# Latent attention: the plain f32 products of two head pairs together in every second slot, and the values of the latents in 64x64 tiles over two banks

## The reference

```python
x = layer_norm(image_embeds, ln1_g, ln1_b)      # the context, 256 rows
l = layer_norm(latents, ln2_g, ln2_b)           # the latents, 64 rows
q = l @ Wq
kv = concatenate([x, l], axis=1) @ Wkv          # 320 rows of keys and values
k, v = split(kv, 2, axis=-1)
w = softmax(einsum('bhqd,bhkd->bhqk', q * scale, k * scale))
out = einsum('bhqk,bhkd->bhqd', w, v)
return out @ Wo                                 # and x = x + this
```

## Time and profile before

| | us |
|---|---|
| median of 3 runs (2218.87 to 2220.65) | 2220.39 |
| the profiled execution | 2218.44 |
| its span, from the first to the last instruction | 2216.6 |
| PE busy in the span | 2118.9 |

### The profile page before, as it was taken

The page is one execution under the profiler, slowest core; times in us unless marked ns, Lnnn a source line. Parts: engine busy times, 40 slices in busy tenths (PEclk is TensorE's granted clock), DMA queues, the critical chain, the costliest instruction groups (busy, mean ns, idle before and its releaser), DMA issues.

```text
span 2216.6 us, 50712 instructions
## 1 busy us (share of the span) xinstructions
PE 2118.9 (96%) x20881; PEld 1883.0 (85%) x20881; DVE 1218.3 (55%) x3619; ACT 1157.9 (52%) x2620; POOL 502.8 (23%) x416
## 2 busy tenths in 40 slices
PE   6999999999999999699879999999999999999999
PEld 5899999998989998466758878878999999999998
DVE  5656565656555555657556777842874843342411
ACT  4656565656565555333237766653444444444443
POOL 0000011000000000122221221232444444444444
PEclk9999999999999999999989999998999999999999
DMA  4000200000000000000031100010101101011000
GB/s 143 21 16 21 72 21 16 23 15 28 18 18 20 16 6 1 11 1 1 1 116 31 31 26 27 12 40 1 58 1 39 39 1 39 1 39 38 1 10 29
DMA packets 48803, 58.08 MB, mean 26 GB/s; under 512 B 6528, under 2 KB 40128, under 8 KB 48448
## 3 DMA queue, kind: packets, MB, share of 16 engines
q1 hardware_dynamic: 48576, 54.85, 7.8%
HBM read 46.72 MB, written 2.10 MB: 22 GB/s over the span
## 4 chain that ended last, share of the span: by engine, by line
PE 45%; DVE 3%; issue 1%; ACT 1%; POOL 0%; POOLq 0%; DVEq 0%; ACTq 0%
PE bank L83 20%; PE bank L1031 16%; PE bank L969 3%; PE bank L955 2%; PE bank L942 1%; PE bank L910 1%; PE bank L978 1%; PE bank L997 1%; DVE dec_room L140 0%; DVE att_rden L1290 0%; DVE att_vz L1272 0%; PE bank L1002 0%; DVE dec_ts_rawa L113 0%; PE bank L901 0%; PE bank L990 0%
## 5 line engine op out<-in xcount | busy, mean ns | idle before, releaser
L861 POOL TENSOR_TENSOR moe_h<-moe_hr,moe_h 128x512 fp32r<-128x512 f32 x256 | 340.8, 1331 | 431.3 <-ACT moe_hr L1175 431.3
L1174 ACT ACTIVATE moe_h<-bank,dec_b 128x512 fp32r<-128x512 f32 x256 | 176.4, 689 | 401.5 <-PE bank L83 378.0
L83 PE MATMUL bank<-lat_wv,lat_kv_t 128*128 128x256 f32 (+1 forms) x1728 | 261.9, 301 | 8.7 <-DVE lat_wv L2188 4.9
L83 PE MATMUL bank<-lat_kv_t,lat_qk 128*128 128x320 f32 x1536 | 258.8, 317 | 0.0
L83 PEld LDWEIGHTS bank<-lat_wv,lat_kv_t 128*128 128x128 f32 x1728 | 224.4, 190 | 16.8 <-ACT lat_v L2096 5.7
L83 PEld LDWEIGHTS bank<-lat_kv_t,lat_qk 128*128 128x128 f32 x1536 | 225.2, 188 | 8.7
L2121 ACT ACTIVATE lat_p<-bank,lat_neg_max 128x320 f32<-128x320 f32 x256 | 135.2, 528 | 166.2 <-DVE lat_neg_max L2237 166.2
L2231 DVE TENSOR_TENSOR lat_qk<-bank,lat_qk 128x256 fp32r<-128x256 f32 x256 | 96.7, 420 | 197.6 <-ACT lat_qk L2115 197.4
L83 PE MATMUL bank<-dec_xt,dec_lo 128*128 128x512 f32 x512 | 202.5, 396 | 0.0
L2237 DVE TENSOR_REDUCE lat_neg_max<-bank 128x1 f32<-128x320 f32 x256 | 125.7, 492 | 132.3 <-PE bank L83 132.1
L1175 ACT ACTIVATE moe_hr<-bank,dec_b 128x512 f32<-128x512 f32 x256 | 174.6, 682 | 0.0
(11 more groups left out here) (321 smaller groups left out, 4060.3 us busy)
## 6 DMA issues: line engine op xcount, KB each, us to landing
raw_w<-in_L_ffn_W SPq DMA_DIRECT2D x16, 1024.0 KB, 6.4
lat_ctx_raw<-in_ctx SPq DMA_DIRECT2D x16, 512.0 KB, 4.0
att_ctx_raw<-in_ctx_turned SPq DMA_DIRECT2D x16, 512.0 KB, 3.7
lat_kv_t<-lat_lt SPq DMA_DIRECT2D x32, 128.0 KB, 2.1
out_x<-x_sb SPq DMA_DIRECT2D x4, 512.0 KB, 2.9
x_sb<-in_x SPq DMA_DIRECT2D x1, 1792.0 KB, 14.7
lat_xl_now<-lat_xl SPq DMA_DIRECT2D x7, 256.0 KB, 4.5
ahead_room<-in_L_xattn_Wq SPq DMA_DIRECT2D x1, 1024.0 KB, 7.3
```

The source lines that it names most:

```text
L83: mm = pe.matmul(out, lhs(a, k), rhs(b, k), start=first and k == 0 and n == 0, stop=last and k == KD - 1 and n == 2)
L861: pool.tensor_tensor(h[:, g % 2, 1, :], hr[:, g % 2, :], h[:, g % 2, 0, :].bitcast(F32), ALU.subtract).then_inc(h_lo, 1)
L1174: act.activation(h[:, n % 2, 0, :], h_bank[n % 2][:, :], ACT.Relu, bias=bias).then_inc(h_hi, 1)
```

## The change

Two steps of each slot are now done for two pairs in every second slot (`s` even), and the program calls the list of a slot's other steps `others`. In an even slot, after v and the extras, stand `o` (the old `weigh`, for pairs `s-2` and `s-1`) and then g (for pairs `s+2` and `s+3`). An odd slot has neither.

- g fills both halves of its two banks, and `qk` becomes a ring of three (`RING`).
- o is a step of the list like the others. It writes entry 0 to `o_bank` and entry 1 to the bank of `proj_bank` whose turn it is. `v_l` is kept once, without zeros, and its product is done on the 64 rows of the entry alone: tiles of 64 rows by 64 columns, one for each entry and head.
- `pt` is kept for two pairs. ACT and DVE read o out in the odd slot after it, in two pieces of 128x128 (two pairs of one entry each): ACT ahead of its exponents, DVE behind its two maxima. They read g out at the end of the even slot, in four pieces of 128x256. DVE's first subtraction now waits for two casts, those of one bank.

```diff
@@
+        def others(pair, s):
+
+
+            n = NU * pair + s
+            steps = [("v", (n + 1) // NU, (n + 1) % NU)] + extras(pair, s)
+            if s % 2 == 0:
+                steps += [("o", (n - 2) // NU, (n - 2) % NU // 2), ("g", (n + 2) // NU, (n + 2) % NU // 2)]
+            return steps
@@
             if kind == "g":
-                return g_lo, 2 * (NU * i + a) + 2
+                return g_lo, 2 * (NU * i + 2 * a + 1) + 2
+            if kind == "o":
+                return o_lo, NU * i + 2 * a + 2
@@
-            pool.memset(v_l[:, :, :], 0.0).then_inc(made, 1)
@@
-            def weigh(c, off, hp):
+            def weigh(c, off, n):
                 i = 2 * c + off
-                if hp % 2 == 0:
-                    pe.wait_ge(v_done, 8 * i + hp + 2)
-                if hp % 4 == 0:
-                    pe.wait_ge(l_done, 2 * i + hp // 4 + 1)
-                wait(pe, o_lo, NU * i + hp)
-                pe.wait_ge(pt_done, 16 * i + 2 * hp + 2)
-                for b in range(2):
-                    for t in range(3):
-                        for h in range(2):
-                            col = hp % 2 * P + h * HD
-                            at_v, at_p = hp * P + h * HD, (2 if t == 2 else 3 * b + t) * P + h * S
-                            of = v_l[:, b, at_v:at_v + HD] if t == 2 else v[:, hp // 2 % 2, 2 * b + t, col:col + HD]
-                            mm = pe.matmul(o_bank[h * HD:(h + 1) * HD, b * S:(b + 1) * S], of, pt[:, at_p:at_p + S],
-                                           start=t == 0, stop=t == 2)
+                pe.wait_ge(v_done, 8 * i + 2 * n + 2)
+                pe.wait_ge(l_done, 2 * i + n // 2 + 1)
+                dst = (o_bank, free_bank(pe, "o", c, off, n))
+                wait(pe, o_lo, NU * i + 2 * n - 1)
+                pe.wait_ge(pt_done, 16 * i + 4 * n + 4)
+                for hp in (2 * n, 2 * n + 1):
+                    at_o = hp % 2 * S
+                    head = lambda h: slice(h * HD, (h + 1) * HD)
+                    for b in range(2):
+                        for t in range(2):
+                            for h in range(2):
+                                col, at_p = hp % 2 * P + h * HD, (3 * b + t) * P + h * S
+                                pe.matmul(dst[b][head(h), at_o:at_o + S], v[:, n % 2, 2 * b + t, col:col + HD],
+                                          pt[:, hp % 2, at_p:at_p + S], start=t == 0, stop=False)
+                    for h in range(2):
+                        for b in range(2):
+                            own, at_v, at_p = slice(b * S, (b + 1) * S), hp * P + h * HD, 2 * P + h * S
+                            mm = pe.matmul(dst[b][head(h), at_o:at_o + S], v_l[own, at_v:at_v + HD],
+                                           pt[own, hp % 2, at_p:at_p + S], start=False, stop=True)
                 mm.then_inc(o_psum, 1)
@@
-                if begun:
-                    weigh(c, *after(off, s, 1))
@@
-                for b in range(2):
-                    own = slice(b * S, (b + 1) * S)
-                    ins = act.copy(v_l[own, b, a * 512:(a + 1) * 512], bank_of("l", c, off, a)[own, :])
-                ins.then_inc(l_done, 1)
+                act.copy(v_l[:, a * 512:(a + 1) * 512], bank_of("l", c, off, a)[:, :]).then_inc(l_done, 1)
@@
-            def query_keys(c, off, hp):
-                n = NU * (2 * c + off) + hp
-                for h, bank in enumerate((g_bank, bank_of("g", c, off, hp))):
-                    dve.wait_ge(g_hi, 2 * n + h + 1)
-                    cols = lambda x: qk[:, hp % 2, x, :, :, h * S:(h + 1) * S]
-                    dve.tensor_tensor(cols(1), bank[:, 0:KD * P].rearrange("p (k b n) -> p k b n", k=KD, b=2), cols(0).bitcast(F32),
-                                      ALU.subtract).then_inc(g_lo, 1)
+            def query_keys(c, off, a):
+                first = NU * (2 * c + off) + 2 * a
+                for h, bank in enumerate((g_bank, bank_of("g", c, off, a))):
+                    dve.wait_ge(g_hi, 2 * first + 2 * h + 2)
+                    for hp in range(2):
+                        n = first + hp
+                        cols = lambda x: qk[:, n % RING, x, :, :, h * S:(h + 1) * S]
+                        src = bank[:, hp * KD * P:(hp + 1) * KD * P].rearrange("p (k b n) -> p k b n", k=KD, b=2)
+                        dve.tensor_tensor(cols(1), src, cols(0).bitcast(F32), ALU.subtract).then_inc(g_lo, 1)
@@
                 maximum(c, off, s, 0)
                 maximum(c, off, s, 1)
-                if not first or g >= 2:
-                    output(c, *after(off, s, 2))
+                if s % 2 == 1 and (not first or g >= 2):
+                    back, hp = after(off, s, 3)
+                    output(c, back, hp // 2)
                 normalise(c, off, s, 0)
                 normalise(c, off, s, 1)
@@
                 nxt, hp = after(off, s, -2)
-                if nxt < 2 or not last:
-                    query_keys(c, nxt, hp)
+                if s % 2 == 0 and (nxt < 2 or not last):
+                    query_keys(c, nxt, hp // 2)
```

More of the change, by code:

```diff
@@ L1665, in latent_attention @@
     COUPLES = NT // 2
+    RING = 3
     with ExitStack() as ctx:
@@ L1737, in in_order @@
                 for s in range(NU):
-                    n = NU * pair + s
-                    steps += [("v", (n + 1) // NU, (n + 1) % NU)] + extras(pair, s) + [("g", (n + 2) // NU, (n + 2) % NU)]
+                    steps += others(pair, s)
             return steps
@@ L1944, in keys_weight, with query_keys @@
                 mm.then_inc(wk_psum, 1)
-            def query_keys(c, off, hp):
+            def query_keys(c, off, n):
                 i = 2 * c + off
[L1949 to L1953, removed]
-                    for h in range(2):
-                        head = slice(h * HD, (h + 1) * HD)
-                        mm = pe.matmul(dst[h][:, kd * P:(kd + 1) * P], wk_t[head, hp, kd * P:(kd + 1) * P],
-                                       q[head, hp, off % 2 * P:(off % 2 + 1) * P], start=True, stop=True)
+                dst = (g_bank, free_bank(pe, "g", c, off, n))
+                wait(pe, g_lo, 2 * (NU * i + 2 * n) - 2)
+                if off % 2 == 0:
+                    pe.wait_ge(q_done, 2 * i + n + 1)
+                for hp in (2 * n, 2 * n + 1):
+                    for kd in range(KD):
+                        for h in range(2):
+                            head = slice(h * HD, (h + 1) * HD)
+                            cols = slice((hp % 2 * KD + kd) * P, (hp % 2 * KD + kd + 1) * P)
+                            mm = pe.matmul(dst[h][:, cols], wk_t[head, hp, kd * P:(kd + 1) * P],
+                                           q[head, hp, off % 2 * P:(off % 2 + 1) * P], start=True, stop=True)
                 mm.then_inc(g_psum, 1)
@@ L2037, in slot @@
                 here = 2 * c + off
-                nxt, hp = after(off, s, -1)
-                nxt2, hp2 = after(off, s, -2)
-                for kind, pair, a in [("v", here + nxt - off, hp)] + extras(here, s) + [("g", here + nxt2 - off, hp2)]:
+                for kind, pair, a in others(here, s):
                     to = off + pair - here
-                    if (first and kind == "w" and pair < 0) or (last and to >= 2):
+                    if (first and kind in "wo" and pair < 0) or (last and to >= 2):
                         continue
                     do[kind](c, to, a)
-                if begun:
-                    weigh(c, *after(off, s, 1))
             def couple(c, first=False, last=False):
@@ L2051, in couple @@
                         slot(c, off, s, first, last)
-            pe.wait_ge(made, 9)
+            pe.wait_ge(made, 8)
             for kind, pair, a in opening:
@@ L2064, in _ @@
             turn(COUPLES - 1, 1, NU - 1)
-            weigh(COUPLES - 1, 1, NU - 1)
+            weigh(COUPLES - 1, 1, NU // 2 - 1)
             project_output(COUPLES - 1, 1, 0)
@@ L2126, in turn, with output @@
                 cols = (0, 2 * P) if n == 0 else (2 * P, 5 * P)
[L2127 to L2131, removed]
+                act.copy(pt[:, hp % 2, cols[0]:cols[1]], pt_bank[n][:, 0:cols[1] - cols[0]]).then_inc(pt_done, 1)
+            def output(c, off, n):
+                act.wait_ge(o_psum, NU // 2 * (2 * c + off) + n + 1)
+                for b, bank in enumerate((o_bank, bank_of("o", c, off, n))):
+                    act.copy(at[:, 0, 2 * n:2 * n + 2, b * S:(b + 1) * S],
+                             bank[:, 0:2 * S].rearrange("p (u n) -> p u n", u=2)).then_inc(o_hi, 1)
             do = {"m": latents_turned, "t": context_turned, "q": queries, "g": query_keys, "v": values, "l": latent_values}
@@ L2324, in _ @@
                 context_split(0, 0, kd)
-            for hp in range(2):
-                query_keys(0, 0, hp)
+            query_keys(0, 0, 0)
             split_weight(2)
```

54 lines of the change are left out of this document (28 added, 26 removed).

## The result

| | before | after |
|---|---|---|
| median of the runs, us | 2220.47 (4 runs) | 2267.69 (4 runs, 2265.89 to 2268.14) |
| profiled execution, us | 2218.44 | 2267.92 |
| span, us | 2216.6 | 2266.1 |

The ratio is 1.0216, with a 95% interval of 1.0202 to 1.023.

A forecast was written before the change was run, and what follows sets the result against it. PE, busy nearly throughout, was taken to bound the kernel. 62 stalls of 1.54 us less 0.14 of gain gave 86.8 us, less 2: +85 on 2218.4, 2303, with 2 for the median 2305 us; range 2268 to 2328.

The forecast's parts named there:

- The wait, its place and its number: In odd slots, v on PE waits for DVE's read-out of o: 62 stalls, 95.5 us in all.
- The length of the wait: Odd slot: v starts at E + 3.86 instead of E + 2.32, so PE stands for 1.54 us.
- E: The start of the odd slot's energies on PE, from which the forecast laid out DVE's queue.
- The energies of an even slot: PE's energies and turn, to the start of v, were taken as 2.33 us in both slots.
- The small waits: PE's waits behind ACT's read-out of v and other work moved at no price: 2 us of gain for all.
- o and g: PE's two steps in the even slot, each for two pairs: o 1.80 us, g 1.12 us.
- the row halves: Latents' products in o: four tiles side by side take 0.12 us a pair, 0.23 if only two run so.
- Rival 1: Stall in odd slots, but free tile changes in o: gain 0.62 us per two slots, 2275 us; chance 0.14.
- the likeliest theory: Stall in odd slots with paid tile changes in o: 2295 to 2330 us; chance 0.74.
- Rival 2: DVE's queue at an odd slot's start is through before PE gets to v: faster, 2180 to 2211 us; chance 0.05.
- Rival 3: The new PE idles bring the stage's granted clock to 0.91: 85 us more, 2390 us; chance 0.05.
- Covers: ACT's exponents come later in odd slots at no price; in even slots o has 0.3 us of cover for `pt`.

The follow-up runs named there:

- e1: The changed kernel with DVE's read-out of o ahead of the two maxima of the odd slot, still behind g's subtractions: 2231.06 us, ratio 1.0058.
- e2: The changed kernel with both read-outs of o, on ACT and DVE, in the even slot ahead of those of g: 2211.71 us, ratio 0.9966.
- e4: The changed kernel with DVE's four subtractions of g behind the two maxima and the read-out of o in the odd slot: 2247.86 us, ratio 1.0132.
- e3: The changed kernel with the latents' products in the 128*64 tile, which also sums the other entry's latents: 2251.81 us, ratio 1.0147.
- e6: e2 with o in the order context, latents, latents, context, so two tile changes within o and not three: 2200.52 us, ratio 0.9912.
- e5: e2 with the context's norm on DVE closed in slot 1 instead of 2 and applied in slot 2 instead of 3: 2196.81 us, ratio 0.9897.

## Why the prediction was right, and where its size was off

- **The wait, its place and its number:** as forecast, 62 times, v behind `lat_at`; the row's total is 55.2 us, and 70 by the starts, where I had 95. e1, e2 and e4 take it away or shorten it in three ways, and in e1 and e4 v starts within 0.02 us of where the queue on DVE puts it. Shown.
- **The length of the wait is the term that was mis-sized:** 1.54 us forecast, 1.13 measured (v at E + 3.46 against the 2.33 of the slot without a wait). ACT's first cast came at E + 0.12 (E + 0.11 forecast) and DVE's first subtraction at E + 0.80 (0.84). The 0.33 that I took for a cast was half of a pair: a cast is 0.39 long, the next starts 0.27 after it, and DVE follows the second by 0.02. The larger error is that I laid DVE's instructions end to end by their lengths, and took 0.38 for a subtraction, again half of a pair. Measured, four subtractions step by 0.33 us, the maxima by 0.40 and the pieces by 0.20, with lengths of 0.42, 0.49 and 0.28. From its first subtraction DVE's chain is 2.61 us instead of 2.97 (3.81 - 0.84), and the first maximum comes at E + 2.13 instead of 2.36. The clue stood in the earlier trace rows: the maximum of 831.30 is 0.49 long, and the next instruction starts at 831.70. I used it once, ahead of the read-out, where it holds for each of the eight instructions. This is 62 x 0.41 = 25 of the 38 us that the forecast was too slow.
- **The energies of an even slot:** I gave both slots the 2.33 us of the earlier trace rows. That is with a change of the tile ahead of it; behind v there is none, and it takes 434.81 - 432.58 = 2.23. I had taken the border off v in the odd slot (1.51 instead of 1.59) but not off the energies behind it: 64 x 0.10 = 6 us.
- **The small waits:** I counted 2 us of gain. Of PE's waits that differ between the two kernels, the new one aside, the kernel before has 19.8 us: 7.4 and 7.0 behind ACT's read-out of v, 2.6 of g on the residual, 1.8 on `pt`, 1.0 of g on `lat_qk`. The changed kernel has 14.2: 8.5, 3.2 and 0.8 behind the read-out of v, 1.0 on `lat_p`, 0.7 on `pt`. The waits on the residual and on `lat_qk` are gone, and the 3.22 us of the earlier trace rows have shrunk: in the changed kernel's first slots PE waits 0.79 and 1.04 us. So some 4 us of the rest of the difference lie here. The last 2 or 3 us stay open. I didn't try these waits one by one.
- **o and g:** 1.77 and 1.10 us against 1.80 and 1.12. The split holds too: three inner borders of 0.14 to 0.16, and the row halves side by side. The Trainium skill's TensorEngine Tiling (Array Packing), section Tiling Modes, says that a change of the tiling mode drains TensorE. The border between 128*64 and 64*64, which the trace of before didn't have, agrees in that it has a price, 0.14 to 0.16 us; that a drain is what is paid for, no run here shows.
- **Rival 1** (free borders) gave 2275 us, nearer to the result than my own sum. Its mechanism is refuted all the same by e3 and e6: right time, wrong cause. The range's low end came from this rival; the likeliest theory alone began at 2295. So it is luck that the result lies at the range's edge and not far below it. By the rival's own terms the low end was 62 x (1.4 - 0.62) = 48, less 2, on 2220.4: 2267 us and not 2268. **Rival 2** fell as a forecast, but its place was right: with the queue in another order (e2) the kernel is faster. **Rival 3:** the granted clock stayed at 1.00 from 45 to 845 us, with idles near 1.1 us.
- **Covers:** I said that ACT's exponents come later at no price. That holds for the changed kernel and fails for e1, e2 and e4. There v waits less or not at all, and the exponents' lateness, which grows by DVE's work of slot 3, reached PE through the read-out of v. For e2 this is shown by e5; for e1 and e4 it is read from where their waits stand, and not tried. I priced the cover for the next energies and for `pt`, not for the read-out of v behind the exponents.

## What to carry to other kernels

When a result takes a buffer of a ring that another step needs, look at where its read-out stands in the in-order programs of the reading engines: here it stood behind six instructions that had nothing to do with it, and moving it beside the next matmuls turned a loss of 47 us into a gain of 7, and of 33 with what followed. Lay such a queue out by the distance from start to start, not by lengths. A smaller tile of the array pays only if what it saves is more than the borders that it brings. Here 16 records saved 0.23 us for two borders or more of about 0.15, so even joined into one stretch they lost; join the stretches of one tile shape, and weigh what is saved against the borders, before making the tiles smaller.

## What the runs showed of the hardware

- A change of the tile of the array between 128*64 and 64*64 costs about 0.15 us: o takes 1.62 us with two such borders and 1.77 with three, and the split of a group of latents gives 0.16. That is as much as ten or eleven records of 64 columns in 64x64 tiles. At the borders of g's 64*128 tile, 16 records take 1.10 us and 8 took 0.65, which leaves 0.20 beyond the records.
- Four 64x64 tiles with two row halves in two banks run at 0.0144 us a record, two 128x64 tiles at 0.0293 (in e3, 16 records in 0.46 us, from 432.68 to 433.14).
- Instructions on DVE and ACT that don't wait start before the one ahead ends by its recorded length: by 0.08 to 0.09 us on DVE in each form here, and ACT's four casts of 128x256, 0.39 long, start 0.27 apart.
